# Where the skip term of a state space layer is added: in the last stage, or as the first summand of the sums over the states

## The reference

```
xn = layernorm(x)
s  = ssm(xn)            # 16 states; see below
g  = silu(moe(xn))      # 8 experts, top 2, capacity 1024 rows per expert
out = x + s * g

ssm: a causal convolution over 4 tokens, silu, projections to delta, B and C,
     h[t,d,n] = exp(delta[t,d] * A[d,n]) * h[t-1,d,n] + delta[t,d] * B[t,n] * x_conv[t,d]
     s[t,d]   = sum over n of h[t,d,n] * C[t,n]  +  xn[t,d] * D[d]
```

## Time and profile before

| | us |
|---|---|
| median of 3 runs (2013.98 to 2049.98) | 2018.49 |
| the profiled execution | 2014.59 |
| its span, first to last instruction | 2012.7 |
| TensorE busy | 1847.6 (92%) |
| VectorE busy | 1853.9 (92%) |
| ScalarE busy | 1222.6 (61%) |
| GpSimd busy | 1303.5 (65%) |

### The profile page before, as it was taken

The page is one execution under the profiler, slowest core; times in us unless marked ns, Lnnn a source line. Parts: engine busy times, 40 slices in busy tenths (PEclk is TensorE's granted clock), DMA queues, the critical chain, the costliest instruction groups (busy, mean ns, idle before and its releaser), DMA issues. The chain is left out here.

```text
span 2012.7 us, 29247 instructions
## 1 busy us (share of the span) xinstructions
PE 1847.6 (92%) x8968; PEld 1449.4 (72%) x8968; DVE 1853.9 (92%) x2004; ACT 1222.6 (61%) x1772; POOL 1303.5 (65%) x621
## 2 busy tenths in 40 slices
PE   6998189999999999999999999999999999999940
PEld 3332078888888878887888788888888888888830
DVE  7998579899998999899989998999899989999899
ACT  3577585556755665566556655666565755675543
POOL 1388466578667776677567866786678667866530
PEclk9999699999999999999999999999999999999975
DMA  9168643346212531244124511351145113621396
GB/s 315 68 97 114 172 173 116 115 162 153 74 64 103 138 86 61 73 146 109 63 73 142 120 68 64 124 121 63 63 150 127 63 63 111 177 74 63 108 355 242
DMA packets 83894, 240.06 MB, mean 119 GB/s; under 512 B 11713, under 2 KB 12609, under 8 KB 71505
## 3 DMA queue, kind: packets, MB, share of 16 engines
q1 hardware_dynamic: 67120, 205.07, 31.1%
q0 software_dynamic: 16416, 33.70, 9.2%
q10 hardware_dynamic: 256, 0.26, 0.1%
HBM read 170.45 MB, written 68.55 MB: 119 GB/s over the span
## 5 line engine op out<-in xcount | busy, mean ns | idle before, releaser
L1188 DVE TENSOR_TENSOR_SCAN a_sb<-a_sb,state,ub_sb 128x512 f32<-128x512 f32 x512 | 894.2, 1785 | 9.9 <-issue 6.0
L1097 POOL TENSOR_TENSOR ub_sb<-u_sb,brow_sb 128x1024 f32<-128x1024 f32 x256 | 629.5, 2459 | 401.7 <-DVE a_sb L1188 398.9
L829 PE MATMUL pm<-xTh,w1l 128*128 128x512 f32 x1024 | 423.0, 413 | 6.8 <-POOL w1l L1082 5.7
L829 PE MATMUL pm<-w2h,hl 128*128 128x512 f32 x1024 | 422.8, 413 | 0.2 <-DVE hl L1168 0.2
L831 PE MATMUL pm<-w2h,hh 128*128 128x512 f32 x1024 | 401.8, 392 | 0.0
L831 PE MATMUL pm<-xTh,w1h 128*128 128x512 f32 x1024 | 401.6, 392 | 0.0
L830 PE MATMUL pm<-w2l,hh 128*128 128x512 f32 x1024 | 398.6, 389 | 0.0
L830 PE MATMUL pm<-xTl,w1h 128*128 128x512 f32 x1024 | 398.1, 389 | 0.0
L1159 DVE SCALAR_TENSOR_TENSOR s_acc_keep<-pt,ct_keep,s_acc_keep 128x512 f32<-128x512 f32 x480 | 352.0, 734 | 19.7 <-PE pt L861 19.0
L976 ACT ACTIVATE a_sb<-delta_sb,neg_a_keep 128x512 f32<-128x512 f32 x512 | 330.2, 713 | 6.7
L861 PE MATMUL pt<-ident_keep,a_sb 128*128 128x128 f32 x2048 | 306.3, 272 | 5.7 <-DVE a_sb L1188 5.7
(11 more groups left out here) (163 smaller groups left out, 1950.8 us busy)
## 6 DMA issues: line engine op xcount, KB each, us to landing
raw_keep<-in_w SPq DMA_DIRECT2D x64, 1024.0 KB, 4.8
brow_sb<-b_chunks SPq DMA_DIRECT2D x128, 256.0 KB
moe_rows<-zeros SPq DMA_DIRECT2D x8, 1280.0 KB, 6.4
xn_rows<-xn_sb SPq DMA_DIRECT2D x8, 1024.0 KB, 9.1
delta_chunks<-ln_sb SPq DMA_DIRECT2D x8, 1024.0 KB
u_chunks<-xn_sb SPq DMA_DIRECT2D x16, 512.0 KB
delta_sb<-delta_chunks SPq DMA_DIRECT2D x8, 1024.0 KB, 8.1
u_sb<-u_chunks SPq DMA_DIRECT2D x16, 512.0 KB, 3.9
```

Of the source, the lines that this page charges most:

```text
L829: pe.matmul(out, sl, mh, start=start, stop=False)
L1097: pool.tensor_tensor(ub[:, h], u[:, 2 * h:2 * h + 2, :], brow[:, m % 2:m % 2 + 1, :].to_broadcast([P, 2, CH]), ALU.mult).then_inc(s_["bmul ...
L1188: op = dve.tensor_tensor_scan(abuf[:, m, 2 * h + k, :], abuf[:, m, 2 * h + k, :], ub[:, h, k, :], state[:, ds(col, 1)], ALU.mult, ALU.add)
```

## The change

The skip term is no longer computed in the last stage. Before a chunk's sums begin, SP loads the chunk's normalised rows from `dr.xn` into `s_acc` (`load_skip`), behind the stores of the chunk before: each load waits until the store of its token block has landed. VectorE multiplies them there with D (`skip`, in steps 3 to 6, one step ahead of the first sum of the token block), and all sums are multiply-adds. The last stage loses `normalise`, `scale` and `add_skip`; the buffers of the ring now hold the last rows of y, and SP issues all 16 loads of y before the first store.

```diff
+                def load_skip(tb):
+                    if begins(e):
+                        sp.wait_ge(s_["x_turned"], TPC + tb + 5)
+                    else:
+                        sp.wait_ge(s_[f"s_out{tb}"], 16 * e)
+                    sp.dma_start(s_acc[:, tb, :], dr.xn[ds(e * CH + tb * P, P)]).then_inc(s_[f"skip_in{tb}"], 16)
...
                     if first and not begins(e):
                         for tb in range(TPC):
                             store_s(tb)
+                    if first:
+                        for tb in range(TPC):
+                            load_skip(tb)
                     for m in range(2, NPQ):
                         load_b(it, q, m)
...
-            for p in range(NP - 4):
+            for p in range(NP):
                 load_y(p)
-            for p in range(2):
-                store(p)
-            for p in range(NP - 2, NP):
-                load_y(p)
-            for p in range(2, 4):
-                store(p)
-            for p in range(NP - 4, NP - 2):
-                load_y(p)
-            for p in range(4, NP):
+            for p in range(NP):
                 store(p)
...
-            for p in range(NP):
-                normalise(p)
             for p in range(NP):
                 silu(p)
...
                 if starts:
-                    dve.wait_ge(s_[f"s_out{tb}"], 16 * e + 16)
-                    dve.tensor_scalar(acc, h, c, None, ALU.mult).then_inc(s_["summed"], 1)
-                else:
-                    dve.scalar_tensor_tensor(out=acc, in0=h, scalar=c, in1=acc, op0=ALU.mult, op1=ALU.add).then_inc(s_["summed"], 1)
+                    dve.wait_ge(s_["skipped"], TPC * e + tb + 1)
+                dve.scalar_tensor_tensor(out=acc, in0=h, scalar=c, in1=acc, op0=ALU.mult, op1=ALU.add).then_inc(s_["summed"], 1)
+
+            def skip(e, tb):
+                dve.wait_ge(s_[f"skip_in{tb}"], 16 * e + 16)
+                dve.tensor_tensor(s_acc[:, tb, :], s_acc[:, tb, :], d_row[:], ALU.mult).then_inc(s_["skipped"], 1)
...
                         if not (first and begins(e) and s < LAG):
                             sum_up(e, q, s, first, last)
+                        if first and LAG <= s + 1 < LAG + TPC:
+                            skip(e, s + 1 - LAG)
                         if s < 8:
                             low_h(it, s)
...
-            scale(0)
-            for p in range(NP):
-                if p + 1 < NP:
-                    scale(p + 1)
-                add_skip(p)
             gate(0)
```

More of the change, by code:

```diff
@@ L646, in main_loop @@
         warm = sb("warm", [P, 2])
-        d_row, shift, zeros = sb("d_row", [P, D]), sb("shift", [P, NT]), sb("zeros", [P, D])
+        d_row, zeros = sb("d_row", [P, D]), sb("zeros", [P, D])
         pm = psum("pm", [P, 4, 512])
@@ L652, in main_loop @@
             b2_in staged add_staged added0 added1 cleared biased carried act_at dve_at pool_at sp_at
-            d_row zeroed shift xn skip whole silu gated sum out
+            d_row zeroed skip_in0 skip_in1 skip_in2 skip_in3 skipped silu gated sum out
             """ + " ".join(f"x_chunk{c} s_chunk{c} y_part{2 * c} y_part{2 * c + 1}" for c in range(NCH)))
@@ L659, in main_loop @@
         y_rows = ([abuf[:, m] for m in range(NPQ)] + [part[:, 0:TPC, :], part[:, TPC:, :]] +
[L660 to L665, removed]
+                  [late[:, 11], ub[:].rearrange("p h k d -> p (h k) d")])
         LAST = NQ * NCH
@@ L784, in _ @@
             for tb in range(TPC):
-                sp.wait_ge(s_[f"s_out{tb}"], 16 * NCH)
+                sp.wait_ge(s_[f"s_out{tb}"], 16 * (NCH - 1))
             sp.wait_ge(s_["exp"], 8 * LAST + 1)
@@ L1016, in _ @@
             chunks(act, chunk)
[L1018 to L1026, removed]
             def silu(p):
@@ L1030, in silu @@
                 act.activation(half(y_rows, p), half(y_rows, p), ACT.Silu).then_inc(s_["silu"], 1)
-            act.wait_ge(s_["shift"], 1)
-            act.wait_ge(s_["l2"], 8 * LAST + 1)
-            act.wait_ge(s_["scan"], 8 * LAST + 2)
-            for p in range(NP):
-                normalise(p)
             for p in range(NP):
@@ L1126, in _ @@
             dve.wait_ge(s_["cleared"], 3)
-            for name, credits in (("x_lo", 2), ("acc_free", 8), ("scan", 2), ("summed", 4), ("biased", 1),
-                                  ("s_out0", 16), ("s_out1", 16), ("s_out2", 16), ("s_out3", 16)):
+            for name, credits in (("x_lo", 2), ("acc_free", 8), ("scan", 2), ("summed", 4), ("biased", 1)):
                 dve.sem_inc(s_[name], credits)
-            mean, rstd = (keep[k][:].rearrange("p c j -> p (c j)") for k in ("mean", "rstd"))
-            dve.scalar_tensor_tensor(out=shift[:], in0=mean, scalar=-1.0, in1=rstd, op0=ALU.mult, op1=ALU.mult).then_inc(s_["shift"], 1)
             def low_x(e, t, bank):
@@ L1154, in sum_up @@
                 if starts:
[L1156 to L1159 removed]
+                    dve.wait_ge(s_["skipped"], TPC * e + tb + 1)
[3 more added lines that the diff above has]
+                dve.tensor_tensor(s_acc[:, tb, :], s_acc[:, tb, :], d_row[:], ALU.mult).then_inc(s_["skipped"], 1)
             for t in range(TILES):
                 low_x(0, t, pm[:, t, :] if t < TPC else pt[:, t - TPC, :])
+            dve.wait_ge(s_["d_row"], 16)
             def chunk(e):
@@ L1209, in _, with gate @@
                 sum_up(NCH, 0, s, True, False)
-            def scale(p):
-                dve.wait_ge(s_["xn"], p + 1)
-                rows = skip_part(p)
-                dve.tensor_tensor(rows, rows, d_row[:].unsqueeze(1).to_broadcast([P, TPP, D]), ALU.mult).then_inc(s_["skip"], 1)
-            def add_skip(p):
-                dve.wait_ge(s_["skip"], p + 1)
+            def gate(p):
                 if p < NP - 2:
                     dve.wait_ge(s_[f"s_chunk{p // 2}"], 16)
-                rows = half(s_rows, p)
-                dve.tensor_tensor(rows, rows, skip_part(p), ALU.add).then_inc(s_["whole"], 1)
-            def gate(p):
-                dve.wait_ge(s_["whole"], p + 1)
                 dve.wait_ge(s_["silu"], p + 1)
```

1 line of the change is left out of this document (removed).

## The result

| | before | after |
|---|---|---|
| median of 4 runs each, us | 2034.24 (2013.98 to 2050.01) | 2045.95 (2043.8 to 2047.64) |
| profiled execution, its span, us | 2014.59, 2012.7 | 2045.24, 2043.4 |
| first matmul of the main loop to the last indirect add, us | 1673.1 | 1722.6 |
| last indirect add to the end of the span, us | 78.5 | 60.6 |
| TensorE's waits in the loop, us | 12.0 | 36.8 |

The change makes the kernel slower by 1.5%: the ratio is 1.0147 [1.0121, 1.0173], in which disturbed runs (two of the four of before are some 35 us above the others) are left out. 2045.95 us is above the range of the forecast, 2006 to 2042. The tail gained 17.9 us, where 17 were forecast. The main loop lost 49.5 us where 27.5 were forecast.

The account below looks back on a forecast made before the run. TensorE was taken to bound the stages, with VectorE following closely. From the profiled 2014.6 us, -17.0 for the tail, +24.5 for chunks 1 to 7 and +3.0 for chunk 0 gave 2025 us, range 2006 to 2042.

Parts of the forecast that it names:

- The tail: After the last indirect add: with `normalise`, `scale` and `add_skip` gone, the span ends 17.1 us earlier, taken as 17.
- The size of TensorE's waits: In the main loop: added waits of 3.5 us in each of chunks 1 to 7, 24.5 us, plus 3.0 in chunk 0.
- the wait at `skip(0)`: Behind step 3's sum, VectorE waits 4.6 us for the load, mostly time lost before too; cost 0.9 us.
- products held by GpSimd: In steps 3 to 6, VectorE's products wait for GpSimd's product as scans do; `skip(3)` about 2 us.
- the late row of B: On SP's queue, `load_b` of m=2 is issued at 910.8 instead of 907.2, landing near 915; GpSimd wants it at 914.5.
- two forms worked out for the row of B: TensorE's step 8 is 3.7 us later, or 2.9 where the row is late and `skip(1)` precedes GpSimd; 3.5 taken.
- the first rival: Products do not wait for GpSimd: 1.9 us a chunk, 15 us in the loop, 2014.6 in all; chance 0.17.
- The reading of the earlier trace: From 345 to 1880 us, where TensorE waits, it waits for VectorE's scans: 8 times, 4.9 us in all.
- the rival: TensorE's clock falls in the new stalls: 1.9 us a chunk, 13 us over seven chunks, 2038; chance 0.05.
- my longest stall is 3.2 us, so I keep the grant at 1.00: TensorE kept full clock about 3.8 us after its last matmul, so stalls of 3.2 us would leave it at 1.00.
- The rival with a late load: At `skip(0)`: load landing beyond about 8.1 us makes the kernel over 2% slower, 2064 at 8.8 us; chance 0.05.
- Its smaller form: At `skip(0)`: a load taking the 4.8 us seen for stores costs 4.8 us a chunk, 2034.

Follow-up runs that it names:

- t8_dose4: Kernel before plus four unused VectorE reductions ahead of the scans of step 6 in chunks 1 to 7; ratio 1.0114.
- t6_place: t2_queue with the products moved, two before the scans of step 4 and two behind those of step 6; ratio 0.9989.
- t7_dose2: Kernel before plus two unused VectorE reductions ahead of the scans of step 6 in chunks 1 to 7; ratio 1.0013.
- t12_wait: Changed kernel with no products, VectorE only waiting for each load, and the row of B issued first; ratio 0.9986.
- t10_adds: t6_place with one of GpSimd's indirect adds done a product later; ratio 0.9931.
- t2_queue: Changed kernel with SP's queue reordered: row of B first, loads of normalised rows interleaved with the stores; ratio 1.0118.
- t4_noload: Changed kernel without the loads of normalised rows in chunks 1 to 7, all products kept; ratio 1.0146.
- t3_tiny: Changed kernel with each product cut to 8 of its 512 columns, waits and loads kept; ratio 1.0137.
- t3b_one: t3_tiny with each 8-column product replaced by a one-operand multiplication by 1; ratio 1.0134.
- t9_rowb: t3_tiny with the row of B issued ahead of the stores; ratio 1.0081.

## Why the prediction was wrong

**The tail** was right: 17.1 us from its own steps, 17.9 measured. The load of y, 32 operations in one piece and 3.3 us at the end came as put down. The table load for `silu`, 1.28 us, was counted behind the load of y; it is done at 1958, long before.

**The size of TensorE's waits** was right, 24.8 us more against 27.5, and so was the mechanism: the three parts that were priced (the wait at `skip(0)`, products held by GpSimd, the late row of B) are all in the trace. Of the two forms worked out for the row of B it was the late one: `skip(1)` slips in ahead of GpSimd and `skip(2)` waits. Inside the sum some things were off. The wait at `skip(0)` was 5.9 us in the chunk shown and 6.2 in the mean, not 4.6: the load took 4.9 us in the chunk shown where I took the stores' 3.6, and over chunks 1 to 7 the first product starts 4.7 to 5.9 us after its load is issued. So `low_h(3)` was late by itself. And the stall came in two pieces, 1.82 and 2.01 us, not in one of 3.2. From 345 us on TensorE waits 31.1 us in all in after and 10.1 us before, so 21.0 us more where 24.5 were put down for chunks 1 to 7. The products were held for 1.93 and 2.70 us (about 2 forecast) in the chunk shown, in chunks 2 and 6 not at all; the first rival, that they never are, has fallen. The reading of the earlier trace rows, that TensorE waits for VectorE's scans where it waits at all, left out the 5.0 us for the weights' low half; the forecast did not hang on it.

**The step that failed** is "my longest stall is 3.2 us, so I keep the grant at 1.00", with its reason in the rival, "3.2 us is under the 3.8, and matmuls stand between the stalls". The 3.8 us of the earlier trace rows are one look at a TensorE that has ended its work; from it I made a bound for stalls within work. The runs deny it: 3.0 us in t8_dose4 bring the clock down in six of seven chunks, and in after, stalls of 1.82 and 2.01 us do. The prediction thus put the clock's term at nothing. The part of the loop's loss that the extra waits leave open is 49.5 - 24.8 = 24.7 us, and 16 pieces at half speed give 27. The rival priced one fall a chunk at 1.9 us, 13 in all, and came to 2038. The measured falls were two a chunk at 1.7 us, 24 us over chunks 1 to 7, and 2025 + 24 = 2049, near the 2045 of the profiled execution. It had a chance of 0.05. It should have had more: a mechanism with a price of its own, of which one row says only that it exists, was excluded by that row.

**The rival with a late load** named a threshold of 8.1 us for the load, above which the whole is over 2% slower. The first load of a chunk stayed below (5.9 us at most) and the whole too. Its smaller form, "4.8 us a chunk, 2034", stood for a load of 4.8 us and did without the clock.

What stays open: what exactly brings the clock down. The stalls of up to 1.9 us in t6_place, t7_dose2 and t12_wait never did, nor did one of 2.18 us in t10_adds. Stalls of about 3.0 us did in 6 of chunks 1 to 7 (t8_dose4); those of 2.6 to 2.8 us in 4 of these chunks in t2_queue and 6 in t4_noload. t3_tiny and t3b_one have nearly the same stalls at step 8 (2.3 to 2.8 and 2.7 to 2.8 us), but the first has falls in 2 of these chunks, the second in 6; in chunk 0 both have one stall of 1.89 us, and only t3b_one has a fall behind it. In after, two stalls of 1.8 to 3.1 us a chunk, 10 us apart, brought one down each, every time. In t9_rowb there are four falls in these chunks: two behind a single stall of 2.32 and 2.25 us, two behind a pair 5.5 us apart. One of these pairs, 1.70 and 2.07 us in chunk 3, is the same to 0.01 us as that of chunk 4, which has no fall. So the length of the stalls alone doesn't decide it, and a stall of 2 to 3 us has to be priced as one that may or may not cost the clock.

## What to carry to other kernels

A stall of the matmul engine has two prices, its length and what the clock takes after it; when stalls of 2 to 3 us are added in a loop, price the second one in the main sum (here 1.7 us for each fall) and look at the granted clock of every chunk's start. An elementwise operation from SBUF to SBUF that is moved beside a busy GpSimd cost the remainder of GpSimd's instruction here, so its place matters more than its size: the same four products cost 38 us in one place and, with the transfers and one add rearranged, 4 in another. And where several causes meet in one place, undoing one shows little; only with all of them undone (queue, place, adds) did the gain of the tail remain.

## What the runs showed of the hardware that I had not expected

- TensorE's clock fell to 0.50 within a main loop in which it is 98% busy, for about 3.4 us at a time, after stalls of 1.82 and 2.01 us. Two pairs of stalls that agree to 0.01 us (t9_rowb, chunks 3 and 4) had a fall in one chunk and none in the other.
- GpSimd can hold a VectorE operation over two of its instructions in a row: 5.58 us for a product of 0.68 us, and 1.91 us for one of 8 columns that takes 0.15. An 8-column `tensor_scalar` with one operand was held for as long as the product with two, 1.97 us in chunk 0.
- A stall of 1.8 us in each of seven chunks cost 1.3 us in all (t7_dose2), while one of 3.0 us in each cost 19.9 (t8_dose4).
